# Moving the LayerNorm apply from GpSimd to VectorE, and one attention eviction from VectorE to ScalarE

## What is computed

```python
def _layernorm(x, axis=-1, eps=1e-5):
    m = jnp.mean(x, axis=axis, keepdims=True)
    v = jnp.var(x, axis=axis, keepdims=True)
    return (x - m) / jnp.sqrt(v + eps)

# attention
q, k, v = per-head projections of x (64 x 64 each)
D = jnp.where(diff >= 0, exp(diff * log(gamma_head)), 0)
ret = ((q @ k.T) * D) @ v
norm = (ret - mean) / sqrt(var + 1e-05) * gn_scale + gn_bias   # per head
gate = x @ w1
out = (gate * sigmoid(gate) + norm) @ w2
# ffn
combine = top-2 of softmax(x @ router_w)
routed = sum_e combine_e * (silu(x @ w1_e) @ w2_e)
shared = sigmoid(x @ shared_gate_w) * ((silu(gate) * up) @ shared_down)

x = x + attn(_layernorm(x))
x = x + ffn(_layernorm(x))
```

## Time and profile before

| | |
|---|---|
| Median of 2 runs | 1988.57 us (1986.49 to 1990.65) |
| The profiled execution, its own time | 1996.72 us |
| Its span, first to last instruction, slowest core | 1995.3 us |
| Spans of the eight cores | 1972.0 to 1995.3 us |
| Busy: PE, DVE, ACT, POOL | 77%, 39%, 19%, 8% |
| Attention with both LayerNorms, to the start of the shared expert | 0 to 817 us |
| Shared expert and experts | 817 to 1995 us |

### The profile page before, as it was taken

The page is one execution under the profiler, slowest core; times in us unless marked ns, Lnnn a source line. Parts: engine busy times, 40 slices in busy tenths (PEclk is TensorE's granted clock), DMA queues, the critical chain, the costliest instruction groups (busy, mean ns, idle before and its releaser), DMA issues.

```text
span 1995.3 us, 20918 instructions; the slowest of 8 cores (1972.0 to 1995.3 us)
## 1 busy us (share of the span) xinstructions
PE 1532.6 (77%) x7156; PEld 617.0 (31%) x7156; DVE 774.7 (39%) x1502; ACT 378.8 (19%) x683; POOL 153.6 (8%) x66
## 2 busy tenths in 40 slices
PE   0565567665674663699899899999999999999960
PEld 0121122121211111244344344444444444443420
DVE  0176447626752662222233232333333333332333
ACT  2423132232233111100021111111111111111100
POOL 1300240042006003000000000000000000000000
PEclk9755665575576556799999999999999999999985
DMA  9000010002000002600311302222130222223015
GB/s 143 2 1 1 0 43 1 0 1 43 1 1 21 1 1 46 103 0 1 58 28 28 51 7 43 43 43 43 16 70 1 43 43 43 43 43 64 0 64 168
DMA packets 41351, 67.26 MB, mean 34 GB/s; under 512 B 3858, under 2 KB 16530, under 8 KB 41250
## 3 DMA queue, kind: packets, MB, share of 16 engines
q0 software_dynamic: 26432, 48.65, 15.3%
q1 hardware_dynamic: 14818, 17.29, 2.7%
HBM read 101.96 MB, written 12.58 MB: 57 GB/s over the span
## 4 chain that ended last, share of the span: by engine, by line
PE 58%; DMA 16%; DVE 10%; issue 7%; POOL 4%; DVEq 3%; ACT 2%; ACTq 0%; SPq 0%; POOLq 0%
PE P L1253 18%; PE P L1285 17%; DMA we_sb<-we 10%; PE P L664 3%; PE P L1118 3%; PE P L1129 3%; PE P L1171 3%; PE P L711 3%; PE P L914 2%; DMA xj<-x 2%; DVE s_sb L695 2%; DMA wgu_sb<-wgu 2%; POOL xlnj L384 2%; DMA x1rl<-x1s 2%; DVEq L881 1%
## 5 line engine op out<-in xcount | busy, mean ns | idle before, releaser
L1253 PE MATMUL P<-x2st,we_sb 128*128 128x512 bf16 x2048 | 452.2, 382 | 10.0 <-DMA we_sb<-we 10.0
L1285 PE MATMUL P<-htil,we_sb 128*128 128x512 bf16 x1984 | 437.6, 382 | 11.0 <-DMA we_sb<-we 11.0
L1264 ACT ACTIVATE hs_scr<-P 128x512 bf16<-128x512 f32 x256 | 152.8, 597 | 773.4 <-PE P L1253 771.2
L1253 PEld LDWEIGHTS P<-x2st,we_sb 128*128 128x128 bf16 x2048 | 199.1, 98 | 255.3 <-issue 24.0
L1285 PEld LDWEIGHTS P<-htil,we_sb 128*128 128x128 bf16 x1984 | 194.7, 98 | 250.0 <-issue 20.2
L1297 DVE TENSOR_TENSOR acc<-acc,P 128x512 f32<-128x512 f32 x248 | 170.6, 688 | 259.0 <-PE P L1285 259.0
L1271 DVE TENSOR_TENSOR htil<-hs_scr,bcomb 128x512 bf16<-128x512 bf16 x256 | 108.9, 425 | 353.3 <-ACT hs_scr L1264 353.3
L449 PE MATMUL P<-xlnj,w1a_sb 128*128 128x512 bf16 x256 | 66.6, 419 | 72.8 <-POOL xlnj L389 71.8
L384 POOL TENSOR_TENSOR xlnj<-xj,bcmu 128x2048 bf16<-128x2048 bf16 x16 | 64.5, 4048 | 631.4 <-DVE bcrs L364 486.9
L711 PE MATMUL P<-s_sb,vst 128*64 128x512 bf16 (+3 forms) x128 | 58.5, 457 | 50.0 <-DVE s_sb L695 50.0
L664 PE MATMUL P<-qt,kst 64*128 64x512 bf16 x128 | 74.9, 598 | 13.1 <-DVE ktok L596 6.1
(11 more groups left out here) (167 smaller groups left out, 1318.5 us busy)
## 6 DMA issues: line engine op xcount, KB each, us to landing
we_sb<-we POOLq DMA_DIRECT2D x16, 2048.0 KB, 14.5
out<-acc SPq DMA_DIRECT2D x4, 2048.0 KB, 8.6
xj<-x POOLq DMA_DIRECT2D x4, 1024.0 KB, 25.9
x1s<-xj SPq DMA_DIRECT2D x4, 1024.0 KB, 5.2
wgu_sb<-wgu POOLq DMA_DIRECT2D x1, 4096.0 KB, 33.7
x1rl<-x1s SPq DMA_DIRECT2D x4, 1024.0 KB, 10.9
w1a_sb<-w1a POOLq DMA_DIRECT2D x1, 2048.0 KB, 23.7
w2a_sb<-w2a POOLq DMA_DIRECT2D x1, 2048.0 KB, 36.1
```

The lines of the kernel that those rows point to most:

```text
L1253: last = e.matmul(bank[:, :], we1_sb[:, 1024 * k + 128 * f:1024 * k + 128 * f + 128], x2st[:, ST * k + 512 * j:ST * k + 512 * j + 512], st ...
L1264: e.activation(hs_scr[:, hsl:hsl + 512], bank[:, :], AF.Silu),
L1285: last = e.matmul(bank[:, :], we2_sb[:, 1024 * f + 128 * m:1024 * f + 128 * m + 128], htil[:, pslot + 512 * f:pslot + 512 * f + 512], star ...
```

## The change

Two edits. In `ln_partB` the four apply instructions go from GpSimd to VectorE, and their order from two subtractions and two multiplications to subtraction and multiplication of the first half, then of the second; this holds for LN1 and LN2 alike. In the head pairs `m_revB` goes from VectorE to ScalarE, behind `m_revA`. The two added lines move everything below down by two.

```diff
-                def a1(e, h):
...
-                m_a1h = [p.do("gpsimd", lambda e, h=h: a1(e, h),
-                              waits=[m_evmu, m_rec, guard] if h == 0 else [],
-                              mark=True) for h in (0, 1)]
-                marks = [p.do("gpsimd", lambda e, h=h: a2(e, h),
-                              waits=[m_a1h[h]], mark=True) for h in (0, 1)]
+                marks = []
+                for h in (0, 1):
+                    def a1(e, h=h):
...
+                    m_a1 = p.do("vector", a1,
+                                waits=[m_evmu, guard] if h == 0 else [],
+                                mark=True)
+                    m_a2 = p.do("vector", a2, waits=[m_a1, m_rec], mark=True)
+                    marks.append(m_a2)
                 prev_lnapply = marks[1]
...
-                    m_revB = p.do("vector", lambda e, c=c: e.tensor_copy(
+                    m_revB = p.do("scalar", lambda e, c=c: e.copy(
                         retj[64:128, 512 * c:512 * c + 512], P[5][64:128, :]),
                         waits=[m_ret_i[3], m_sq_prev[c % 2]], mark=True)
                     m_rev = m_revB
-                    m_retj_ev[c] = Mark("m_vector", m_revB.value)
+                    m_retj_ev[c] = m_revB
```

More of the change, by code:

```diff
@@ L381, in ln_partB, with a2 @@
                 in3 = xj[:, xoff:xoff + 4096].rearrange("p (c t) -> p c t", t=512)
-                def a1(e, h):
[L383 to L391, removed]
-                m_a1h = [p.do("gpsimd", lambda e, h=h: a1(e, h),
-                              waits=[m_evmu, m_rec, guard] if h == 0 else [],
-                              mark=True) for h in (0, 1)]
-                marks = [p.do("gpsimd", lambda e, h=h: a2(e, h),
-                              waits=[m_a1h[h]], mark=True) for h in (0, 1)]
+                marks = []
+                for h in (0, 1):
+                    def a1(e, h=h):
+                        with nc.allow_low_precision(reason="bf16 LN apply"):
+                            return e.tensor_tensor(mid[:, 4 * h:4 * h + 4, :],
+                                                   in3[:, 4 * h:4 * h + 4, :],
+                                                   mu_b, ALU.subtract)
+                    def a2(e, h=h):
+                        with nc.allow_low_precision(reason="bf16 LN apply"):
+                            return e.tensor_tensor(out3[:, 4 * h:4 * h + 4, :],
+                                                   mid[:, 4 * h:4 * h + 4, :],
+                                                   rs_b, ALU.mult)
+                    m_a1 = p.do("vector", a1,
[3 more added lines that the diff above has]
+                    marks.append(m_a2)
                 prev_lnapply = marks[1]
```

## The result

| | before | after |
|---|---|---|
| Median | 1991.1 us (10 runs) | 1908.49 us (11 runs) |
| The profiled execution | 1996.72 us | 1906.05 us |
| Its span, slowest core | 1995.3 us | 1904.5 us |
| First reciprocal (L364) to the shared expert's first matmul | 754.88 us | 670.24 us |
| From there to the end | 1178.01 us | 1175.52 us |

What follows compares the result with a forecast made beforehand. Most time was the experts' matmuls and weight loads, untouched; TensorE's 117 us of waits for GpSimd's apply were the target. 11.0 + 56.1 + 19.2 + 1 = 87.3 us off 1988.6 gives 1901 us, range 1880 to 1928.

Steps and rivals of the forecast that it cites:

- The apply's price: LN1 and LN2: one 2048-column apply instruction takes 1.23 us on VectorE, four 5.1 us instead of 16.2 on GpSimd.
- the first rival: Apply on VectorE: the repeated tile costs the double rate, 2.3 us an instruction, 1925 us in all; chance 0.10.
- the third: Apply on VectorE: slow in itself like the reciprocal, up to 13.4 us an instruction, 2280 us in all; chance 0.02.
- the fourth: Apply on VectorE: costs as much as on GpSimd, 4.05 us an instruction, gaining 8 us, 1980 us; chance 0.04.
- The third rival's line: Whole kernel: apply instructions of duration a, 32 of them, are worth about 138 - 32a us, turning at 4.3 us.
- LN1 of block 0: Gate chunks 4 to 7 of block 0 can start at about 71.1 instead of 82.12 us, gaining 11.0 us.
- Blocks 1 to 3: LN1 with the previous block's LN2: gate chunk 2 gains 10.7 us, the first pair 8.0; three blocks 56.1 us.
- LN2 of block 3 and the load: Router ends 11.05 us earlier and `wgu_sb`'s load, issued early, lands before that; shared expert gains 19.2 us.
- the second rival's first half: `wgu_sb`'s load starts no earlier or is slow beside x1's store; with costlier ScalarE queueing 1920 us, chance 0.08.
- The second edit: Head pairs, eviction on ScalarE: 0.2 us gained in 21 pairs, 0.3 lost at block 3's 7 and four block ends.
- The sum: Whole kernel: the terms add to 87.3 us less, 1901 us from the runs' median of 1988.6.
- What was to be seen: Profile signs: apply 1.2 us, gate wait 28, router wait near 9, values' wait gone, small Silu wait, early `wgu_sb` load.

Runs made afterwards that it cites:

- the full-width tiles: Changed kernel with the two spread tiles, mean and reciprocal deviation, in fp32 instead of bf16: 1932.43 us, ratio 0.9694 to the kernel before.
- The load held back: Changed kernel with the load of `wgu_sb` also waiting for LN2's apply: 1919.27 us, ratio 0.9644 to the kernel before.
- the apply alone: Changed kernel with the second eviction back on VectorE, both applies staying on VectorE: 1910.81 us, ratio 0.9567 to the kernel before.
- the second eviction alone: Kernel before with only the second eviction moved to ScalarE, applies on GpSimd: 2030.48 us, ratio 1.0109, its profiled run disturbed.

## Why the prediction was right

**The apply's price** was the term on which all else hung, with bounds from 0.43 to 13.4 us, and 1.23 us taken; 1.21 to 1.23 measured. That excludes the first rival, the third and the fourth. Of the reason given, the full-width tiles show that the type decides: the same instruction with an fp32 tile takes 2.27 us. That the repeated tile costs nothing follows from the measured 1.21 us being no more than the 1.23 worked out for a plain operand; no run has a plain one of 2048 columns beside it. The third rival's line, 138 - 32a, is too steep: at the measured price it would have given 99 us, and the full-width tiles cost 25.2 us for 1.07 us more an instruction, 24 times and not 32, since most of LN2's apply lies beside the gate: its four instructions made the first pairs only 1.0 to 1.3 us longer. The Trainium skill's rule on repeated rows (Vector Engine (DVE) Microarchitecture Reference, 5.1 Performance modes) is borne out by the 1.21 us. Its table of modes (VectorE: DVE Perf Modes, The perf-mode tier table) gives 1224 ns for this operation on 2048 elements in bf16 and 2293 ns in fp32; the traces agree with 1206 to 1226 and, for one fp32 operand of the two, 2273.

**LN1 of block 0**: 11.0 predicted; reciprocal to first projection went from 35.11 to 24.00 us, 11.1.

**Blocks 1 to 3**: 56.1 predicted. Up to the gate's end 10.87 each instead of 10.7, with the gate released by ScalarE's Silu, as foreseen. The first pairs gained 8.48, 8.11 and 7.43 instead of 8.0 each. Together 56.6.

**LN2 of block 3 and the load**: 19.2 predicted. From the last reciprocal to the shared expert 53.44 became 34.35 us, 19.1. The load held back shows that the early issue is 6.8 us of it, and so that the second rival's first half was excluded for the reason given. Held, the place still gained 12.0 us, where the prediction had 11.0 or less, since the transfer took 32.5 us there and not 33.9. The 0.5 us taken for the barrier had no row behind them; 0.8 were measured.

**The second edit** is the mis-sized term: "I take 0.2 gained in each of the 21, because the values' matmuls eat a good half of VectorE's lead", in all 1 us gained. It lost 2.2 us: the pairs behind the first gained 0.59, 0.26 and 0.70 us in blocks 0 to 2, lost 2.58 in block 3 (9.64 a pair instead of 9.20, 0.43 against 0.3 foreseen), and the block ends, with block 0's first pair, lost 1.21. The 1.2 foreseen for them is luck rather than a reading: block by block the ends came out between 1.1 us longer and 0.5 us shorter, and their sum differs by 1.5 us between the cores of the changed kernel. The 4.2 us of gain are what was not there: 1.55 came, 0.09 us a pair. Part of the reason is in the rows of the apply alone: ScalarE's second eviction makes the square 0.42 us later, not 0.3, which is what block 3 pays in every pair; and in the pair shown 0.35 of VectorE's 0.50 us are eaten, which leaves 0.15, not 0.2. Why it is less still over all pairs (0.04 against the apply alone, 0.12 with the second eviction alone against before) is not shown. The stages of the apply alone and of the second eviction alone agree in direction, with 2.4 and 3.0 us lost. The prediction called itself wrong if pairs grew by over 0.3 us; in block 3 they grew by 0.43, so in this term it was.

**The sum**: 11.1 + 56.6 + 19.1 - 2.2 = 84.6 us, against 87.3; that it is the stage's 84.64 is no test, since the terms divide the stage up. So 2.7 of the 7.5 us between 1901 and 1908.5 are accounted for by these terms. Another 2.5 are the starting point, 1988.6 from two runs where ten gave 1991.1; the rest is within what medians of a few runs differ (the interval of the ratio alone is 14 us wide). The experts' stage, which should not have changed, did not by the mean of the cores.

**What was to be seen** came so: gate wait 26.4 us (28 foreseen), router wait 8.7 (9), the load issued 40 us before the router's end, the values' wait gone. One sign was weak: TensorE's wait for ScalarE's gate eviction came to 2.0 us in all where it had been 0.9, and before gate chunk 2 of block 2 it is 0.22 us, as in the earlier trace rows. ScalarE's queue does set that start, but TensorE is ready hardly earlier. And a pair of blocks 1 and 2 became 0.09 us shorter, not 0.2.

## What to carry to other kernels

Before an elementwise step is moved to another engine, its price there can be worked out from a shorter row of the same operation, types and memory, as fixed part and price per column; one operand of another type nearly doubled it here, so look at every operand, the small repeated one too. A move frees a queue as well as an engine: here the earlier transfer was worth a third of what its site gained. Where two engines evict side by side, giving both halves to one of them lengthens the chain of eviction, square and sum, and the freed engine's lead is kept only if nothing it needs stands behind that chain.

## What the runs showed of the hardware

An operand that is a 512-column bf16 tile read four times costs VectorE no more than what is worked out for a plain one (1.21 us for 2048 columns against 1.23 from the 0.426 us row); making that one operand fp32 costs 1.07 us, nearly as much again.

On ScalarE two independent copies don't always overlap: L346 begins 0.49 us after L345, which takes 0.57, while the two evictions of 64 partitions each, which take 0.58, begin 0.60 us apart. The first pair of rows, from the stretch of block 2 shown above:

```profile
389.98 0.57 ACT L345 CAST stat_b<-P 1x512 bf16<-1x512 f32 x1
390.47 0.61 ACT L346 CAST stat_b<-scrF 1x512 bf16<-1x512 f32 x1
```

The Trainium skill (ScalarE: Activation LUTs, What ACT_TABLE_LOAD costs) has back-to-back ACTIVATEs overlap by about 93 ns; these two rows, which are copies, agree with about 80 ns, the evictions show none. L345 reads PSUM and L346 SBUF, and the two are one group, but neither is the reason alone: L360 and L335, two groups that both read PSUM, start 0.48 us apart in the same block, though L360 takes 0.58. What makes the difference was not tried.
